# Local-attention layers: inverse lengths by Ln and Exp, softmax factors inside the exponential, a rotary sum in one operation, and a new order

## What is computed

```
for i in range(DEPTH):                                   # 6
    x = attn_layer(shift_tokens(x), ...) + x
    x = ffn_layer(shift_tokens(x), ...) + x
attn_layer: q, k, v = split(x @ Wqkv)                    # 16 heads of 64
    q, k = l2norm(q) * qs, l2norm(k) * ksc               # l2norm: t / max(norm(t), 1e-12)
    q = q * cos * scale + rotate_half(q) * sin * scale
    k = k * cos / scale + rotate_half(k) * sin / scale
    local_attention: windows of 32 tokens; each looks at its own window and the one before
    attn = softmax(where(mask, -max, q k^T * 8)); out = (attn v) @ Wo
ffn_layer: layer norm, W1 (128 -> 2 x 341), a * gelu(gate), W2
```

## Time and profile before

| what | value |
|---|---|
| time, median of 3 runs | 5307.67 us (5293.55 to 5323.05) |
| the profiled execution's own time | 5290.19 us |
| its span, first to last instruction | 5288.8 us |
| TensorE's mean granted clock | 0.949 of full speed |
| local layers | from about 895 to 3950 us |

### The profile page before, as it was taken

How to read it: one execution, slowest core, us unless ns; L and a number is a source line. 1 busy time by engine, 2 the same in 40 slices (tenths; PEclk the granted TensorE clock), 3 DMA queues, 4 the chain that set the end, 5 groups by cost and what they waited for, 6 DMA issues and landing times. The chain is left out here.

```text
span 5288.8 us, 145626 instructions
## 1 busy us (share of the span) xinstructions
PE 4739.1 (90%) x60536; PEld 3208.5 (61%) x60536; DVE 4452.8 (84%) x9387; ACT 3689.8 (70%) x6571; POOL 2927.2 (55%) x3441
## 2 busy tenths in 40 slices
PE   6999997999899999999999899999987999968878
PEld 3333333777777777777777777777764555544445
DVE  7989996999999999889999999999976777577665
ACT  2888885777777787777777777777763677735522
POOL 2121003878887887777788878878762011024624
PEclk6999998999999999999999999999996999989989
DMA  0000100000000000000000000000000000000000
GB/s 23 1 1 1 32 5 24 26 10 11 13 26 10 11 16 26 11 8 15 26 11 8 31 10 11 13 10 10 8 19 10 2 2 2 2 16 1 1 1 16
DMA packets 51748, 63.45 MB, mean 12 GB/s; under 512 B 12820, under 2 KB 41258, under 8 KB 50322
## 3 DMA queue, kind: packets, MB, share of 16 engines
q1 hardware_dynamic: 51090, 54.14, 3.4%
HBM read 25.17 MB, written 4.19 MB: 6 GB/s over the span
## 5 line engine op out<-in xcount | busy, mean ns | idle before, releaser
L1548 POOL TENSOR_TENSOR x<-x,b_norm 128x512 f32<-128x512 f32 x768 | 793.8, 1054 | 389.4 <-DVE b_norm L1413 377.7
L1162 PE MATMUL psum<-b_w_vo,b_mixed 128*128 128x128 f32 x6144 | 798.0, 279 | 10.2 <-ACT b_mixed L1278 4.3
L1162 PEld LDWEIGHTS psum<-b_w_vo,b_mixed 128*128 128x128 f32 x6144 | 756.3, 194 | 68.7 <-ACT b_mixed L1278 44.1
L652 DVE TENSOR_REDUCE a_top<-psum 128x1 f32<-128x512 f32 x1024 | 637.7, 682 | 79.8 <-PE psum L471 77.5
L583 ACT ACTIVATE a_prob<-psum 128x512 f32<-128x512 f32 x1024 | 557.1, 606 | 119.6 <-PE psum L487 111.7
L1278 ACT COPY b_mixed<-psum 128x512 f32<-128x512 f32 x768 | 435.4, 594 | 248.7 <-PE psum L1147 248.6
L1233 ACT ACTIVATE b_square<-psum 128x512 f32<-128x512 f32 x768 | 462.6, 602 | 186.1 <-PE psum L1085 182.3
L1539 POOL TENSOR_TENSOR x<-x,b_cross 128x256 f32<-128x256 f32 x768 | 565.0, 736 | 14.3 <-DVE b_cross L1397 14.3
L1541 POOL TENSOR_TENSOR x<-x,b_cross 128x256 f32<-128x256 f32 x768 | 568.3, 740 | 0.0
L1405 DVE TENSOR_REDUCE b_norm<-b_square 128x8 f32<-128x512 f32 x768 | 508.2, 663 | 44.9 <-ACT b_square L1233 38.2
L1555 POOL TENSOR_TENSOR x<-x,b_stat 128x512 f32<-128x512 f32 x384 | 405.7, 1069 | 237.6 <-DVE b_stat L1442 234.1
(11 more groups left out here) (334 smaller groups left out, 11262.5 us busy)
## 6 DMA issues: line engine op xcount, KB each, us to landing
b_prev<-b_xs_x SPq DMA_DIRECT2D x24, 384.0 KB, 3.4
ab<-in_L_ffn_Wqkv SPq DMA_DIRECT2D x6, 1024.0 KB, 5.1
b_shifted_x<-y SPq DMA_DIRECT2D x24, 224.0 KB, 2.6
b_shifted_f<-y SPq DMA_DIRECT2D x48, 112.0 KB, 2.1
ab<-in_L_ffn_Wqkv SPq DMA_DIRECT2D x6, 512.0 KB, 6.5
ab<-in_L_ffn_Wo SPq DMA_DIRECT2D x6, 512.0 KB, 7.7
b_prev<-b_xs_x SPq DMA_DIRECT2D x24, 112.0 KB, 3.4
x<-in_L_attn_x SPq DMA_DIRECT2D x4, 512.0 KB, 7.6
```

The source lines that it names most:

```text
L652: e.tensor_reduce(top2[i % 2][:, t, c, head:head + 1], banks[n][:, 0:wide], AX.X, ALU.max).then_inc(emptied[n], 1)
L1162: made = e.matmul(banks[n][:, 0:D], mixed[:, h, :], w_vo[l % 2][:, h, :], start=h == 0, stop=h == 2 * PAIRS - 1)
L1548: e.tensor_tensor(rh, rh, bcast(norm[i % 2][:, 1, HPC * c:HPC * (c + 1)], 2, LDIM), ALU.mult).then_inc(sem["scaled"], 1)
```

## The change

Inverse lengths: the squared sums go straight into `bounded` and are bounded by 1e-24 (VectorE), then Ln with a factor 2^16 and Exp with -0.5 (both ScalarE) give the inverse length; the rotary tables carry a factor 2^8 to make up for it. The layer norm's root is done in the same way. q is no longer scaled (`scale` has c 2 and 3 only): its inverse lengths stand as a per-partition scale in the exponential, which becomes one operation for each head and bank, 128x64, with a bias (the negative maximum times the inverse length) and a scale, read from PSUM. `less` is now that product of 128x8, both operands from SBUF. The rotary sum is one POOL operation; the sign moves into the table. The table with Exp and Ln is set at the start and after each Gelu. All times of the order are new.

```diff
-NORM_BEGINS, NORM_STEP, APPLY_BEGINS, APPLY_STEP, BIAS_BEGINS = 8.765, 1.266, 10.333, 0.800, 49.998
-MOVE_X, PLACE_X, MOVE_F, PLACE_F, SHIFT_CUT = 1.750, 54.592, 42.751, 62.162, 112
+NORM_BEGINS, NORM_STEP, APPLY_BEGINS, APPLY_STEP, BIAS_BEGINS = 14.363, 0.327, 2.993, 0.039, 74.433
+MOVE_X, PLACE_X, MOVE_F, PLACE_F, SHIFT_CUT = 21.319, 60.536, 46.833, 71.461, 112
-    project=(-0.002, 3.321, 8.470, 11.414), square=(-1.301, 5.108, 8.467, 12.070), rope=(1.152, 8.473, 9.866, 13.650),
-    sum_squares=(4.429, 8.939, 10.808, 12.956), add=(49.249, 50.075, 53.022, 62.918), invert=(13.389, 14.189, 14.669),
-    scale=(59.819, 60.760, 61.187, 64.837), turn=(19.024, 22.116, 24.753, 27.221), copy_turned=(18.206, 22.225, 23.304, 27.927),
-    score=(27.447, 29.946), top=(29.521, 30.157), less=(31.773, 32.372), exp=(32.689, 33.303),
-    sum=(33.308, 34.708), invert_sum=(33.534, 35.014), weigh=(77.530, 77.548), block=(36.490, 37.009),
-    gather=(41.441,), spread=(43.596, 43.599, 44.821, 45.084), out=(48.224, 48.769, 49.749, 50.713), join=(50.789,))
+    project=(-4.745, 3.534, 8.828, 9.338), square=(-2.725, 0.680, 9.274, 10.280), rope=(-0.301, 1.863, 5.206, 10.002),
+    sum_squares=(3.197, 5.060, 9.448, 9.950), add=(52.266, 55.662, 58.085, 63.946), invert=(11.777, 15.159, 15.759),
+    scale=(65.584, 67.007), turn=(20.056, 25.054, 25.290, 27.117), copy_turned=(19.862, 21.833, 25.355, 29.442),
+    score=(30.694, 35.854), top=(31.885, 32.638), less=(32.487, 32.851), exp=(33.405, 33.920),
+    sum=(34.012, 34.464), invert_sum=(34.316, 34.684), weigh=(85.449, 86.717), block=(34.846, 36.000),
+    gather=(41.245,), spread=(42.745, 42.959, 43.674, 45.692), out=(53.565, 53.661, 53.729, 55.863), join=(50.639,))
-REST = 0.560
-FF_PIECES = dict(fill=(15.214, 17.707, 22.975), empty=(14.498, 17.493, 21.387))
+REST = 0.206
+FF_PIECES = dict(fill=(18.355, 22.030, 24.345), empty=(15.755, 18.111, 20.398))
...
                 if kind == "turn":
-                    q.wait_ge(sem["scaled"], nth["scale", i, c])
+                    if c < 2:
+                        q.wait_ge(sem["roped"], nth["add", i, c])
+                    else:
+                        q.wait_ge(sem["scaled"], nth["scale", i, c])
...
-                    e.activation(bounded[i % 2][:, :, 0], norm[i % 2][:, 0, :], ACT.Sqrt).then_inc(sem["inverted"], 1)
+                    if step[2] == 1:
+                        made = e.activation(nm[:, 1, :], nm[:, 0, :], ACT.Ln, scale=SQUARES_UP)
+                    else:
+                        if i > 1:
+                            q.wait_ge(sem["lessened"], 2 * (i - 1))
+                        made = e.activation(nm[:, 1, :], nm[:, 1, :], ACT.Exp, scale=-0.5)
...
-                    e.activation(pr[:, :, :, :], pr[:, :, :, :], ACT.Exp).then_inc(sem["powered"], 1)
+                    q.wait_ge(sem["lessened"], nth["less", i, c])
+                    if i:
+                        q.wait_ge(sem["blocked"], nth["block", i - 1, c])
+                    for h in range(HPC):
+                        made = e.activation(prob[c][:, :, h, :], scores[:, :, h, :], ACT.Exp, bias=stat[j % 4][:, 0, h:h + 1],
+                                            scale=norm[i % 2][:, 1, 2 * h + c:2 * h + c + 1])
+                    made.then_inc(emptied[n], 1)
...
-                    e.activation(chip.spread[:, slot_of, tiles, 0], chip.mean_var[:, slot_of, tiles, 1],
-                                 ACT.Sqrt).then_inc(sem["norm_parts"], 1)
+                    if part == NORM_ROOT:
+                        made = e.activation(chip.spread[:, slot_of, tiles, 0], chip.mean_var[:, slot_of, tiles, 1], ACT.Ln)
+                    else:
+                        made = e.activation(chip.spread[:, slot_of, tiles, 1], chip.spread[:, slot_of, tiles, 0], ACT.Exp,
+                                            scale=-0.5)
...
                     e.activation(hidden[:], hidden[:], ACT.Gelu).then_inc(sem["gelu"], 1)
+                    e.preload_act_table_set("natural_log_exp_and_others")
...
-                    if step[2] == 1:
-                        made = e.tensor_reduce(nm[:, 0, :], bounded[i % 2][:, :, :], AX.X, ALU.max)
-                    else:
-                        made = e.reciprocal(nm[:, 1, :], nm[:, 0, :])
+                    e.tensor_reduce(norm[i % 2][:, 0, :], bounded[i % 2][:, :, :], AX.X, ALU.max).then_inc(sem["inverted"], 1)
...
                 if kind == "less":
+                    q.wait_ge(sem["inverted"], INVERT_PARTS * (i + 1))
+                    e.tensor_tensor(stat[j % 4][:, 0, :], stat[j % 4][:, 0, :], norm[i % 2][:, 1, c:LHEADS:2],
+                                    ALU.mult).then_inc(sem["lessened"], 1)
-                    e.tensor_tensor(prob[c][:, :, :, :], banks[n].rearrange("p (s h k) -> p s h k", s=2, h=HPC),
-                                    per_head(stat[j % 4][:, 0, :]), ALU.subtract).then_inc(emptied[n], 1)
...
-                    e.tensor_tensor(rh[:, :, 0:half], rh[:, :, 0:half], xh[:, :, half:LDIM],
-                                    ALU.subtract).then_inc(*chain.step())
-                    e.tensor_tensor(rh[:, :, half:LDIM], rh[:, :, half:LDIM], xh[:, :, 0:half],
-                                    ALU.add).then_inc(sem["roped"], 1)
+                    e.tensor_tensor(turned, turned, crossing[:, :, ::-1, :], ALU.add).then_inc(sem["roped"], 1)
```

More of the change, by code:

```diff
@@ L812, in local_order @@
             for c, time in enumerate(times):
-                put(i, time, kind, i, c)
+                put(i, time, kind, i, 2 + c if kind == "scale" else c)
         if b == BATCH - 1 and l + 1 < DEPTH:
@@ L996, in local_stage @@
         prob_t = sb("prob_t", [2, 2 * PAIRS, WINDOW])
-        stat = [sb(f"stat{n}", [3, HPC]) for n in range(4)]
+        stat = [sb(f"stat{n}", [2, HPC]) for n in range(4)]
         hidden = sb("hidden", [len(FBLOCKS), BANK])
@@ L1233, in scalar_ @@
                     e.activation(square[r % 2], banks[n], ACT.Square).then_inc(sem["squared"], 1)
-                if kind == "invert" and step[2] == 0:
-                    q.wait_ge(sem["summed"], all_of("sum_squares", i))
-                    q.wait_ge(sem["inverted"], INVERT_PARTS * i)
-                    e.activation(bounded[i % 2][:, :, 0], norm[i % 2][:, 0, :], ACT.Sqrt).then_inc(sem["inverted"], 1)
+                if kind == "invert" and step[2] > 0:
+                    nm = norm[i % 2]
+                    q.wait_ge(sem["inverted"], INVERT_PARTS * i + step[2])
+                    if step[2] == 1:
[4 more added lines that the diff above has]
+                        made = e.activation(nm[:, 1, :], nm[:, 1, :], ACT.Exp, scale=-0.5)
+                    made.then_inc(sem["inverted"], 1)
                 if kind == "copy_turned":
@@ L1310, in scalar_ @@
                                  bias=b1[0:size, part, f, l:l + 1]).then_inc(emptied[n], 1)
-                if kind == "norm" and step[4] == NORM_ROOT:
+                if kind == "norm" and step[4] in (NORM_ROOT, NORM_ROOT + 1):
                     l, b, h, part = step[1:]
@@ L1346, in norm_part @@
                         made = e.scalar_tensor_tensor(out=var, in0=var, scalar=EPS_LN, in1=var, op0=ALU.add, op1=ALU.max)
-                    elif part == NORM_ROOT + 1:
-                        made = e.reciprocal(root, tmp)
                     else:
@@ L1441, in vector_ @@
                     q.wait_ge(sem["totalled"], nth["sum", i, step[2]])
-                    e.reciprocal(stat[j % 4][:, 2, :], stat[j % 4][:, 1, :]).then_inc(sem["sums"], 1)
+                    e.reciprocal(stat[j % 4][:, 1, :], stat[j % 4][:, 1, :]).then_inc(sem["sums"], 1)
                 if kind == "block":
@@ L1472, in vector_ @@
                                       banks[n].rearrange("p (a d) -> p a d", a=4)).then_inc(emptied[n], 1)
-                if kind == "norm" and step[4] != NORM_ROOT:
+                if kind == "norm" and step[4] not in (NORM_ROOT, NORM_ROOT + 1):
                     l, b, h, part = step[1:]
@@ L1501, in gpsimd_ @@
             for n in range(2):
-                e.memset(bounded[n][:, :, 1], 1e-12).then_inc(sem["cleared"], 1)
+                e.memset(bounded[n][:, :, 1], LEAST_SQUARES).then_inc(sem["cleared"], 1)
             q.wait_ge(sem["dma_small"], 176)
+            e.tensor_scalar(less_scale[:, :, :, :], qk_scale[:, :, :, LDIM // 2:LDIM], -1.0, None,
+                            ALU.mult).then_inc(*chain.step())
+            q.wait_ge(*chain.now())
             for step in order:
@@ L1510, in gpsimd_ @@
                         q.wait_ge(emptied[at], roped)
+                    first, second = slice(0, LDIM // 2), slice(LDIM // 2, LDIM)
                     for k in (0, 2):
-                        for half in (slice(0, LDIM // 2), slice(LDIM // 2, LDIM)):
-                            made = e.tensor_tensor(table[:, t, k:k + 2, half], base_table[:, t, k:k + 2, :],
-                                                   bcast(qk_scale[:, k // 2, l, half], 1, 2), ALU.mult)
```

(11 more changed lines are left out.)

41 lines of the change are left out of this document (22 added, 19 removed).

## The result

The changed kernel takes 5768.35 us in the median (5763.48 to 5769.21), against 5307.59 before: a ratio of 1.0866, 95% interval 1.0843 to 1.0889. It is slower, as forecast, but by 461 us and not by 96, and the time lies above the range. The span of its profiled execution is 5762.2 us.

What follows compares the result with a forecast made beforehand. VectorE's own lap was taken to bind the kernel before, 15.9 us per tile. The new lap through TensorE and the exponentials, 15.9 plus 0.5, gave 192 x 0.5 = +96 us: 5404 us, range 5200 to 5540.

Steps and rivals of the forecast that it cites:

- Rival A: The lap through the exponentials binds: +0.25 to +1.0 us per tile, 5355 to 5500 us; chance 0.48.
- the ring through the softmax: Lap from gather through the next scores, VectorE's softmax and ScalarE's exponentials to the next gather; forecast 16.4 us per tile.
- Together 0.6, of which I take 0.5: Extras on the new lap, in us per tile, reduced since they partly fall together; they make 15.9 into 16.4.
- the bare chain of 15.9 us: New lap per tile: softmax chain 8.9, hand-over 0.2, TensorE's part 6.4, plus 0.43 of unexplained waits.
- Gelu's term: Gelu with two loads, about 4 us, ahead of the first exponential once in eight tiles, some 2 counted: 0.2 per tile.
- That lap is slack and VectorE's own lap is what binds: Kernel before: TensorE's lap through the softmax takes 14.0 of 15.9 us per tile; VectorE's maximum-to-maximum lap takes 15.89.
- POOL's gain at nothing: POOL's work falls from 12.7 to 8.9 us per tile (single rotary sum, two scalings fewer), counted as no time gained.
- The table loads: ScalarE loses 1.8 loads per tile, 2.3 us; in front of Sqrt or Exp they end almost no wait.
- Rival B: Faster because the exponentials are cheaper: at a step of 0.2 us TensorE limits, 15.4 per tile, 5212 us; chance 0.25.
- Rival C: POOL holds up `less`, which reads two SBUF operands, by one POOL operation, 1.05 us per tile: 5606 us; chance 0.12.
- The three extras: Per tile on the new lap: feed-forward banks emptied between exponentials 0.25, layer norm's Ln 0.2, Gelu with its loads 0.2.
- my bare sum of 14.0: Old TensorE lap per tile: 4.9 gather to scores, 8.5 softmax, 0.2 handing over, 0.4 unexplained waits; against 15.9.

Runs made afterwards that it cites:

- gelu_no_loads: The changed kernel with Square in place of Gelu and without the table set behind it: 5623.95 us (1.0609).
- less_one_operand: The changed kernel with a reciprocal of 128x8 in place of the product of two SBUF operands in `less`: 5713.58 us (1.0769).
- exp_whole: The changed kernel with one exponential of 128x512 per bank, constant scale, no softmax bias or inverse lengths of q: 5223.60 us (0.9849).
- old_ops_new_order: The kernel before, all its operations kept, with the order tables of the changed kernel: 5503.68 us (1.0389).
- the single maximum: The kernel before with Ln and Exp, one maximum per bank as bias of one 128x512 exponential, no `less`: 5268.45 us; in the new order 5265.62 us.
- add_split: The changed kernel with the rotary sum again in two POOL operations of 128x256: 5754.85 us (1.0854).
- ln_exp_and_add: The kernel before, old order, with Ln and Exp for Sqrt and reciprocals and the single rotary sum: 5308.55 us (1.0019).
- ln_exp_only: The kernel before, old order, with Ln and Exp in place of Sqrt and reciprocals alone: 5303.64 us (1.0004).

## Why the prediction was right in kind and wrong in size

- **The mechanism.** Rival A, named the likeliest, is what happened: sixteen exponentials in a row come to lie on the ring through the softmax. The step was forecast as 0.29 us and measured as 0.293; VectorE's wait for them as 1.6 us and measured as 1.6; ScalarE's work 13.5 and 13.7. Removing the pointers removes 528 us.
- **The step that failed** is the last one of the section on the order: "Together 0.6, of which I take 0.5". What the laps have beyond the bare chain of 15.9 us is 2.4 us, not 0.5, and 1.9 x 192 = 365 us is the error. The kinds of tile divide it, as means over all 191 laps: the Gelu tiles are 21.09 - 16.94 = 4.15 us longer than plain ones, which is 1.0 per tile where I had 0.2; the root tiles are 1.35 longer, 0.33 where I had 0.2; the plain tiles themselves take 16.94 and not 15.9, 1.04 where I had 0.25 for emptied banks.
- **Gelu's term** was wrong in its path as well as in its size. I counted only the Gelus that stand ahead of the first exponential, and half of their time as idle. In the trace 23 of 46 stand there, and in their laps it is 3.95 us from the first maximum to the first exponential, where plain laps have 1.29. The other 23 stand behind the exponentials, ahead of the copies that TensorE's turns and scores need; in their laps it is 2.74 us from transpose to gather instead of 0.23, and 8.66 to the end of the scores instead of 7.06. Both kinds of lap take 21.1 us. gelu_no_loads shows that the loads are what does it.
- **In the plain tiles** the excess of 1.04 lies between first maximum and first exponential (0.4 more than forecast, and less_one_operand takes 0.25 off a plain lap: the hold of `less`), and among the exponentials (5.28 us, where sixteen in a row take 4.83: banks emptied between them, forecast as 0.25). The rest is a few tenths that no run explains. TensorE's part of a plain lap is as forecast, 6.85 us to the start of the last score matmul.
- **TensorE's clock** is no explanation that the runs bear out. It was 0.96 in the mean against 0.99 before and 1.00 from 2000 to 3000 us in exp_whole, where TensorE's part of the ring is 6.71 us instead of 7.24; but in old_ops_new_order it is 1.00 too, and TensorE's part is 7.40.
- **"That lap is slack and VectorE's own lap is what binds"** doesn't stand. Ln and Exp took 0.25 us of VectorE's work per tile away and the time stayed; with the single maximum it was 1.26, and 0.2 came of it. Before the change, too, VectorE's own work is not what binds. That the rings through several engines do is what remains, and which of them is open. With it falls the frame of my sum, which gave the new lap 1.9 us of slack to use up first.
- **POOL's gain at nothing:** right for the rotary sum, shown by add_split and by ln_exp_and_add; that the two scalings of q are worth nothing no run tested by itself. The single sum's 1.06 was too low (1.29), without effect: I took the row of a multiplication, where a sum of 128x512 stood in the same trace at 1286 ns.
- **The table loads** in front of Sqrt and Exp: their removal, with VectorE's 0.25 us, came to 0.04% with an interval of 0.15% in ln_exp_only. That agrees with the forecast as a sum, and partly by luck, since plain tiles gained and Gelu tiles lost.
- **Rival B** (the exponentials cheaper): wrong in its premise, the step was 0.293. Its figure was 5212 for a step of 0.2; the run without pointers, at a step of 0.105, gave 5241. So the floor under the lap was put nearly right, if a little low.
- **Rival C** acts, with a quarter of the price given to it.
- **The range.** Its upper end of 5540 is 232 us above the kernel before, 1.2 us per tile of extras. The three extras were averages over the tiles, cut down by idle time, as if they could still fall into the slack that the same change was taking away.

## What to carry to other kernels

A per-partition bias or scale of an activation is paid per instruction: to split one wide activation into many narrow ones with pointers, count the pointers first, 16 x 2 x 0.09 us here, and set them against what they replace on the same ring, not against busy time of other engines. Where several in-order engines pass a tile around, take each stretch of the ring as a mean over all tiles of the old kernel and not from one tile: the softmax took 9.25 us in the mean where the tile I read showed 8.5, and the 1.9 us between my bare sum of 14.0 and the real 15.9 were in part no slack but the same hold-ups that came back as the error. And work that comes in one tile of four (here a Gelu with its two loads, 4.05 us in a row) has to be followed on every ring that it stands in front of, at its full length, before it is averaged.

## What the runs showed of the hardware

- Activations of 128x64 from PSUM follow one another at 0.105 us with constants, at 0.293 us with a bias and a scale read per partition; one alone takes 0.278 and 0.435 us.
- A VectorE product of 128x8 with both operands in SBUF took 131 to 1309 ns while POOL was busy 55% of the time; the 269 of 384 that took 250 ns or more all began while a POOL operation ran and ended 19 to 29 ns after the end of one. A reciprocal of the same size, with one operand, took 162 to 205 ns, also while POOL ran.
- POOL sums of 128x512 took 1.29 us, whether the halves of one operand are exchanged by a negative step (1286 ns) or not (1286 to 1287); products with an operand repeated along the row took 1.05 to 1.07.
- Removing 340 table loads, with two small Exps added 390 us less for ScalarE, changed nothing in the sum; removing the 96 around Gelu in the changed kernel, 123 us, gave 144 us.
